# Attention of all 49 tiles in a loop of its own in the first ten steps, its result and the input kept in place of the tile's transposed input

## The reference

```
Wh  = xn @ W + b;  gnn[d] = mean of Wh[src] over the 100000 edges with that dst       (graph part)
q,k = elu(xn @ wq + bq) + 1, elu(xn @ wk + bk) + 1;  v = xn @ wv + bv                 (8 heads of 32)
mix = (q @ (k^T v)) / (q . sum(k) + 1e-6) @ wo + bo                                   (linear attention)
x1  = x + gnn + mix
out = x1 + expert MLP of layernorm(x1)     (top 1 of 8 experts, 256 -> 1024 -> 256, capacity 977, softmax weight)
```

## Time and profile before

| | |
|---|---|
| median of 3 runs | 1505.08 us |
| the profiled execution | 1504.29 us |
| its span | 1502.5 us |
| mean granted TensorE clock | 0.875 |
| TensorE matmuls busy | 1147.8 us (76%) |
| GpSimd busy | 961.9 us (64%) |
| VectorE busy | 833.8 us (55%) |
| ScalarE busy | 558.1 us (37%) |

### The profile page before, as it was taken

One profiled execution on the slowest core, in us unless ns is written; L12 is line 12 of the kernel. 1 busy time (PEld: TensorE's weight loads), 2 busy tenths in 40 slices (PEclk: granted clock), 3 DMA queues, 4 the chain that ended last, 5 costly groups with the idle time before them and its releaser, 6 DMA issues.

```text
span 1502.5 us, 33191 instructions
## 1 busy us (share of the span) xinstructions
PE 1147.8 (76%) x5962; PEld 790.6 (53%) x5963; DVE 833.8 (55%) x3074; ACT 558.1 (37%) x1460; POOL 961.9 (64%) x969
## 2 busy tenths in 40 slices
PE   3779876456565556588888888988899999988796
PEld 2557543122222223365656656666666767767685
DVE  6755333033233235356566766777777777776454
ACT  4832211011111113243434544555444545554342
POOL 5447777777777767777776776767767767611111
PEclk9589997566677668899999999999999999999898
DMA  7583334344344443545455554555555545534452
GB/s 238 190 263 99 104 101 134 102 131 133 103 148 143 135 123 114 166 142 168 143 174 174 178 171 138 176 169 168 183 181 182 188 156 177 164 101 132 136 182 84
DMA packets 141735, 228.94 MB, mean 152 GB/s; under 512 B 29856, under 2 KB 86723, under 8 KB 141618
## 3 DMA queue, kind: packets, MB, share of 16 engines
q0 software_dynamic: 42800, 115.65, 25.2%
q1 hardware_dynamic: 97454, 111.65, 23.5%
q10 hardware_dynamic: 1364, 0.54, 0.2%
HBM read 194.65 MB, written 34.81 MB: 153 GB/s over the span
## 4 chain that ended last, share of the span: by engine, by line
PE 29%; POOL 27%; issue 27%; DMA 6%; POOLq 4%; DVE 3%; ACT 2%; SPq 1%; ACTq 0%; DVEq 0%; PEldq 0%
POOL shared L594 26%; PE pY L1055 7%; PE pH L1064 7%; PE pA L935 5%; DMA shared<-table,idx 4%; PE pQ L1001 1%; PE pX L1032 1%; PE pX L1028 1%; DMA shared<-in_L_ffn_b_dram 1%; PE pX L1030 1%; PE pD L938 1%; PE pH L912 1%; DMA shared<-in_x_dram 1%; POOLq L554 1%; POOLq L562 1%
## 5 line engine op out<-in xcount | busy, mean ns | idle before, releaser
L594 POOL DMA_INDIRECT shared<-table,idx x784 | 811.3, 1035 | 299.4 <-issue 255.2
L935 PE MATMUL pA<-shared,onehot 128*128 x976 | 304.1, 442 | 238.4 <-POOLq L571 173.3
L935 PEld LDWEIGHTS pA<-shared,onehot 128*128 x976 | 102.5, 105 | 429.4 <-issue 381.4
L1055 PE MATMUL pY<-w2s,shared 128*128 x832 | 196.6, 390 | 11.9 <-issue 9.0
L1064 PEld LDWEIGHTS pH<-shared 128*128 128x128 f32 x1664 | 193.9, 192 | 2.6
L1064 PE MATMUL pH<-shared 128*128 128x128 f32 x1664 | 194.3, 275 | 0.0
L707 ACT ACTIVATE shared<-pA,rdeg 128x256 f32<-128x256 f32 x49 | 23.2, 473 | 437.0 <-DVE rdeg L1493 433.1
L1055 PEld LDWEIGHTS pY<-w2s,shared 128*128 128x128 f32 x832 | 157.0, 194 | 33.9 <-issue 13.7
L1481 DVE CUSTOM_DVE_ANT_1 pD<-pD,ident 128x512 f32<-128x512 f32 x49 | 34.3, 700 | 210.9 <-PE pD L941 198.7
L772 ACT ACTIVATE shared<-pH,b1s 128x128 f32<-128x128 f32 x416 | 116.2, 371 | 49.6 <-PE pH L1064 47.0
L531 POOL DMA_INDIRECT out_dram<-shared,jtok x52 | 55.7, 1072 | 114.0 <-issue 114.0
(11 more groups left out here) (275 smaller groups left out, 1744.0 us busy)
## 6 DMA issues: line engine op xcount, KB each, us to landing
shared<-in_L_ffn_w_dram SPq DMA_DIRECT2D x104, 512.0 KB
shared<-table,idx POOLq DMA_INDIRECT x784
w2s<-in_L_ffn_w_dram SPq DMA_DIRECT2D x8, 1024.0 KB, 6.5
rows<-rows_sb SPq DMA_DIRECT2D x7, 1040.0 KB, 14.9
shared<-rows SPq DMA_DIRECT2D x52, 130.0 KB
shared<-in_L_ffn_b_dram SPq DMA_DIRECT2D x52, 128.0 KB
shared<-in_x_dram SPq DMA_DIRECT2D x12, 512.0 KB, 8.7
table<-w2s SPq DMA_DIRECT2D x12, 512.0 KB, 3.5
```

What stands on the lines that cost most here:

```text
L594: g.indirect_dma_start(gathered[:, s * G + j, :], None, table[:, :], bass.IndirectOffsetOnAxis(ap=idx[:, q * G + j:q * G + j + 1], axis=0) ...
L935: m = pe.matmul(pA[:, :], onehot[:, n % OQ, j, :], groups[:, f % RQ, j, :], start=False, stop=stop)
L1055: ins = pe.matmul(pY[:, 0:D], hs[:, c, :], w2s[:, bass.ds(e * FC * D + c * D, D)], start=(c == 0), stop=(c == FC - 1))
```

## The change

The attention leaves the steps of its tiles. It runs in a loop of its own, `attend`, six tiles in each of the steps 0 to 4, four in each of 5 to 8, and the last three in step 9. TensorE does query(b+1), divisor(b), the projection of tile b-1 (`mixed`, which takes the bias and the `ms` matmuls out of `project_sum`), and spread(b). ScalarE does the Relu of b+1, the divisors' copy of b behind the projection of b-1, and the Exp of b+1. VectorE adds the projection to the input tile and keeps it in the tile's place in `xts` (`attended`), which isn't needed any more, adds the 8 gate columns to `xgs`, and does qn and qf. The banks change: divisors to pH0, spread to pH1, projection to pY, which no job uses yet. Input tiles come in pairs into a part of `hs`, which jobs use from step 10 on, and `xres` is gone. In a step with attention, VectorE's `place` and `combine` stand ahead of it and the next tile's one-hots behind it; TensorE's attention stands between `count` and `turn_sums`. The core of the diff:

```diff
+SIX = 5
...
+        xpair = hs[:, 0:2 * DK, :].rearrange("p (a c) n -> p a (c n)", a=2)
...
-        xres = part_of(D)
...
+        def attended(t):
+
+            return xts[:, bass.ds(t, 1), :, :].rearrange("p t k n -> p (t k n)")
...
+            def load_res(a, par, first=False):
+
+                if not first:
+                    sp.wait_ge(S["at_ok"], a)
...
+            with sp.Fori(1, SIX) as t:
+                load_pairs(3 * t, 3 * t + 3)
                 step(t, False, False, False)
                 load_out_weights(t)
+            with sp.Fori(SIX, T0 - 2) as t:
+                load_pairs(2 * t + SIX, 2 * t + (SIX + 2))
+                step(t, False, False, False)
+                load_out_weights(t)
...
+            def attend(b):
+
+                more = not isinstance(b, int) or b + 1 < NT
+                if more:
+                    a.wait_ge(S["qf_ok"], b + 1)
                     a.sem_inc(S["act_hold"], 1)
+                    a.wait_ge(S["q_ps"], b + 2)
+                    query_part(qr, ACT.Relu)
+                a.wait_ge(S["rd_ok"], b + 1)
                 a.sem_inc(S["act_hold"], 1)
+                if not isinstance(b, int) or b >= 1:
+                    a.wait_ge(S["at_ps"], b)
+                    a.sem_inc(S["act_hold"], 1)
                 each = rden[:, :].rearrange("p (h a) -> p h a", a=1).broadcast_to([P, HEADS, HD])
                 a.activation(qn.rearrange("p (h d) -> p h d", h=HEADS), each, ACT.Copy).then_inc(S["dn_ok"], 1)
+                if more:
+                    query_part(qe, ACT.Exp).then_inc(S["qe_ok"], 1)
...
+                def mixed(t):
+
+                    pe.wait_ge(S["qn_ok"], t + 1)
+                    pe.sem_inc(S["pe_hold"], 1)
+                    pe.wait_ge(S["at_ok"], t + 1)
+                    pe.sem_inc(S["pe_hold"], 1)
+                    pe.matmul(pY[:, 0:GW], qn[:, 0:P], ms[:, 0, :], start=True, stop=False)
+                    pe.matmul(pY[:, 0:D], two16[:, :], bo16[:, :], start=False, stop=False)
+                    pe.matmul(pY[:, 0:GW], qn[:, P:D], ms[:, 1, :], start=False, stop=True).then_inc(S["at_ps"], 1)
+
+                def attend(b):
+
+                    inner = not isinstance(b, int)
+                    if inner or b + 1 < NT:
+                        pe.wait_ge(S["qe_ok"], b + 1)
+                        pe.sem_inc(S["pe_hold"], 1)
+                        query(b + 1).then_inc(S["q_ps"], 1)
+                    divisor(b)
+                    if inner or b >= 1:
+                        mixed(b - 1)
+                    spread(b)
...
-                    pe.matmul(pX[:, 0:GW], st[:, 0:P], wgs[:, 0, :], start=True, stop=False)
-                    pe.matmul(pX[:, 0:D], two16[:, :], bo16[:, :], start=False, stop=False)
-                    pe.matmul(pX[:, 0:GW], st[:, P:D], wgs[:, 1, :], start=False, stop=False)
                     for m in range(DK):
-                        ins = pe.matmul(pX[:, 0:GW], qn[:, m * P:(m + 1) * P], ms[:, m, :], start=False, stop=(m == DK - 1))
+                        ins = pe.matmul(pX[:, 0:GW], st[:, m * P:(m + 1) * P], wgs[:, m, :], start=(m == 0), stop=(m == DK - 1))
...
+                def keep(t, landed_at, par):
+
+                    v.wait_ge(S["at_ps"], t + 1)
+                    hold(v, "dve_hold")
+                    v.wait_ge(S["xo_in" if par else "xe_in"], landed_at)
+                    hold(v, "dve_hold")
+                    v.tensor_tensor(attended(t), pY[:, 0:D], xpair[:, par, :], ALU.add)
+                    at = xgs[:, bass.ds(t, 1), :].rearrange("p t n -> p (t n)")
+                    v.tensor_tensor(at, pY[:, D:GW], at, ALU.add).then_inc(S["at_ok"], 1)
+
+                def attend(i, par):
+
+                    t = 2 * i + par
+                    inner = not isinstance(t, int)
                     k = part("share_c", t)
+                    v.wait_ge(S["den_ps"], t + 1)
+                    hold(v, "dve_hold")
+                    k(v.tensor_scalar(rden[:, :], pH0[:, 0:HEADS], 1e-6, None, ALU.add))
                     assert k.n == K["share_c"]
                     v.reciprocal(rden[:, :], rden[:, :]).then_inc(S["rd_ok"], 1)
+                    if inner or t >= 1:
+                        keep(t - 1, i * 16 + 16 if par else i * 16, 1 - par)
                     v.wait_ge(S["qf_ok"], t + 1)
                     hold(v, "dve_hold")
                     v.wait_ge(S["rx_ps"], t + 1)
                     hold(v, "dve_hold")
+                    v.tensor_tensor(qn, qf, pH1[:, 0:D], ALU.mult).then_inc(S["qn_ok"], 1)
+                    if inner or t + 1 < NT:
+                        queries(t + 1)
...
+                    if pairs:
+                        if inner or t >= 2:
+                            place(t - 2)
+                        combine(t)
...
+                            attend_pairs(*pairs)
...
                     if inner or t + 1 < NT:
                         next_tile(t)
```

More of the change, by code:

```diff
@@ L363, in _, with load_pairs @@
             sp.dma_start(bgb, gnn_b.partition_broadcast(P)).then_inc(S["bg_in"], 16)
[L364 to L371, removed]
-                else:
-                    sp.dma_start(xres, x_t[bass.ds(t, 1), :, :].rearrange("t p d -> p (t d)")).then_inc(S["xr_in"], 16)
+            def load_res(a, par, first=False):
+                if not first:
+                    sp.wait_ge(S["at_ok"], a)
+                    hold(sp, "sp_hold")
+                name = "xo_in" if par else "xe_in"
+                if isinstance(a, int) and a == NT - 1:
+                    sp.dma_start(xpair[0:LAST, par, :], x[(NT - 1) * P:N, :]).then_inc(S[name], 16)
+                else:
+                    sp.dma_start(xpair[:, par, :], x_t[bass.ds(a, 1), :, :].rearrange("t p d -> p (t d)")).then_inc(S[name], 16)
+            def load_pairs(lo, hi):
+                with sp.Fori(lo + 1, hi + 1) as i:
+                    load_res(2 * i, 0)
+                    load_res(2 * i + 1, 1)
             def store_x1(t, last=False):
@@ L774, in hidden, with step @@
                     ins.then_inc(S["h_sb"], 1)
-            def step(t, turn=True, work=True, out_=True):
+            def step(t, turn=True, work=True, out_=True, pairs=None):
                 inner = not isinstance(t, int)
@@ L782, in step @@
                     count_on(t)
[L783 to L786, removed]
+                if pairs:
+                    if isinstance(t, int) and t == 0:
+                        attend(0)
+                        attend(1)
+                        attend_pairs(1, pairs[1])
+                    else:
+                        attend_pairs(*pairs)
+                    if isinstance(t, int) and t == T0 - 1:
+                        attend(NT - 1)
                 if turn:
@@ L797, in step @@
                     softmax(t - 1)
[L799 to L803, removed]
+            a.wait_ge(S["q_ps"], 1)
+            query_part(qr, ACT.Relu)
+            query_part(qe, ACT.Exp).then_inc(S["qe_ok"], 1)
+            step(0, False, False, False, (0, 3))
+            with a.Fori(1, SIX) as t:
+                step(t, False, False, False, (3 * t, 3 * t + 3))
+            with a.Fori(SIX, T0 - 1) as t:
+                step(t, False, False, False, (2 * t + SIX, 2 * t + (SIX + 2)))
+            step(T0 - 1, True, False, False, (2 * (T0 - 1) + SIX, (NT - 1) // 2))
             step(T0, True, True, False)
@@ L1094, in step @@
                         ins.then_inc(S["px_ps"], 1)
-                    if inner or t < NT:
-                        pe.wait_ge(S["qf_ok"], t + 1)
-                        pe.sem_inc(S["pe_hold"], 1)
-                        if inner or t + 1 < NT:
-                            query(t + 1)
-                        divisor(t).then_inc(S["qd_ps"], 1)
+                    if pairs:
+                        if isinstance(t, int) and t == 0:
+                            attend(0)
+                            attend(1)
+                            attend_pairs(1, pairs[1])
+                        else:
+                            attend_pairs(*pairs)
+                        if isinstance(t, int) and t == T0 - 1:
+                            attend(NT - 1)
+                            mixed(NT - 1)
+                            pe.wait_ge(S["at_ok"], NT + 1)
                     if out_:
@@ L1620, in step @@
                         node_out(t - 1)
-                    if inner or t < NT:
-                        divisors(t)
-                    if inner or t >= 2:
+                    if not pairs:
                         place(t - 2)
```

116 lines of the change are left out of this document (62 added, 54 removed).

## The result

The changed kernel takes **1582.2 us** (median of 4 runs, 1575.7 to 1589.8) against 1506.5 before: ratio 1.049, 95% interval 1.046 to 1.052. It is slower where 1483 us was forecast, outside the range, and of the other sign.

The account below looks back on a forecast made before the run. GpSimd's issue of gathers was taken to bound the first ten steps and nearly the next 14 tiles, TensorE the last 24. Early +44, middle -15, late -48, tail -2 gave -21 us from 1504.3: 1483 us, range 1454 to 1522.

Parts of the forecast that it names:

- So I take 2.4 GHz: Early attention loop: TensorE at work 2.9 of 4.4 us, a larger share than in an earlier stretch, so full clock.
- rival (b): Early attention loop: TensorE falls to 1.2 GHz, trips of 5.9 us, +69 us, 1552 us in all; chance 0.05.
- The round trip, 4.4 us: Early steps: each further attention costs one pass round three engines, 4.4 us, ends 4.1 and 5.0.
- (a): Early attention loop: dearer handovers, trips of 5.3 us, early stage 41 us more, 1524 us in all; chance 0.21.
- The end of a loop: Early steps: VectorE's last two products, leaving the loop and the next tile's one-hots keep TensorE waiting 3.8 us.
- Late steps: Last 24 tiles: TensorE loses 2.7 us a step, to 14.8 or 16.4; VectorE bounds three-group steps at 15.8.
- The term of -48: Last 24 tiles: 383 us in place of 431, 48 us less.
- GpSimd's 362 us stay below: Last 24 tiles: GpSimd needs 272 x 1.33 = 362 us, less than the 383 us forecast for the stage.
- The -15 of the middle stage: Tiles 10 to 24: GpSimd sets the pace at 291 of 306 us, so only its 15 us can go.
- The tail: Behind the last node sum, mostly expert jobs: 147.2 us becomes 145, a change of -2 us.
- (d): Late steps hardly shrink since VectorE keeps 17 us: 12 us saved in place of 48, 1519 us; chance 0.04.
- (c): Early attention hides better behind GpSimd, 4.0 us each: early stage costs 20 in place of 44, 1459 us; chance 0.13.

Follow-up runs that it names:

- e1: Changed kernel with two matmuls on zeros per attention, filling TensorE's wait for ScalarE: 1544.2 us, ratio 1.026.
- e2: Changed kernel with a job's weights loaded ahead of the next job's rows in SP's queue: 1586.4 us, ratio 1.052.
- e17: Changed kernel in which GpSimd sends out no finished job inside the steps, 39 instructions less: 1573.7 us, ratio 1.045.
- e4: Changed kernel with the divisors' copy in its own buffer and VectorE's addition to the input behind the next query: 1518.7 us, ratio 1.009.
- e18: Changed kernel with the whole attention left out, VectorE only copying the input tiles: 1477.2 us, ratio 0.981.
- e5: Changed kernel with each group's rows scattered three groups behind its gathers instead of five: 1613.9 us, ratio 1.069.

## Why the prediction was wrong

**"So I take 2.4 GHz"** failed first. The forecast argued from one stretch of the earlier trace rows, where TensorE was at work for 3.06 of 6.8 us at 2.4 GHz, that a larger share of work would hold that clock. The stretches above show that share says little: at 1.2 GHz TensorE was at work for 29.4 of 33.0 us, at 2.4 GHz for 17.6 of 22.8. Of 39 trips between two spreads of one loop 19 took over 6 us. That is 19 x 2.1 = 40 us, and e1 gave back 38. e2 and e17 have 20 and 19 such trips, but partly in other steps: which loops fall to 1.2 GHz isn't fixed by the step. It is rival (b), given 0.05, in half of the trips. (b) was sized as +69 for all steps with trips of 5.9 us; they took 6.7. The Trainium skill (TensorE: Matmul & The Clock Gate, section "A second HAM failure mode: psum-queue depth-cycling") had warned of short idles between groups of matmuls. The loops at 1.2 GHz bear out its warning, but not its picture of a clock that swings between the levels as the idles recur: here it kept one level for five trips on end in steps 0, 3 and 4, and changed within a loop in steps 1, 2 and 9.

**The round trip, 4.4 us**, was well built. Measured 4.56: divisors 0.44 for 0.37, the projection to ScalarE's start 1.68 for 1.54, then to the spread 0.56 (0.56), to L1550 0.55 (0.54), from there to L1522 0.75 for 0.56, to the next divisors 0.57 (0.54); the 0.3 for handovers is in these. The query's 1.22 for 0.97 lies beside it. The forecast counts a trip 46 times, but its own steps hold 39 behind the first attention of each, so in the ends of its range and in the sizes of (a) and (b) the trips weigh a sixth too much; 0.16 x 39 = 6 us were missed here. **The end of a loop**, 3.8 us from the first of VectorE's two last products to the first group, was 4.8 (L1550 at 474.19, L972 at 479.02): 10 us in ten steps. Part of both came back in the groups behind, 12.2 us for 13.1 in step 3. The four steps at 2.4 GHz throughout (3, 4, 6, 8) took 158.7 us where the forecast has 154.6, and with the filler all ten took 437.3 for 423. So 38 of the 52 us at tile 10 are the clock, and 14 are what is left with the clock held: trips and ends above their price.

**"Late steps"**: the 2.7 us of TensorE were right (14.90 measured for 14.8; 16.7 to 17.3 for 16.4). VectorE's 15.8 us as the next bound was wrong: it kept up with 14.9. The term of -48 failed by another step: **"GpSimd's 362 us stay below"**. In the last stage GpSimd is busy for 299.8 us, and 0.30 us stand between two of its 274 instructions: 382 us in which it waits for nobody, 10 more than the 372 of TensorE. It isn't below; it is the slower of the two. Its instructions are dearer here (1.09 us busy) than in the early stretch from which 1.33 us each was taken (211.04 / 210, 1.00 us). The difference sits in 23 of its 267 indirect transfers: they took 1.87 to 3.13 us, each of them beside one of VectorE's 24 one-hots (L1489, 2.29 us), and the other 244 took 0.98. That is 36 us; in the last stage of the kernel before it is 18 transfers and 22 us. Two engines near one pace, a few groups of ring between them, and a scatter that one of them issues between gathers: waits stay, and 382 became 415. How these 33 us of waits arise is argued from the chain above, and no run takes them away: in e1, e4 and e18 GpSimd's sum is 375 to 378 us and the stage 410 to 413. The forecast named TensorE waiting for rows or expert weights behind GpSimd's scatters as a thing that would be wrong, but priced it at nothing. In e17, with GpSimd at 259.2 + 248 x 0.30 = 334 us, 19 us came back; in e5, with the scatter moved, the wait moved too.

**The -15 of the middle stage** became -8, and this though TensorE came into it with a full ring, which is worth 12 us (310.4 in e18, 298.3 after) and with which the forecast had 282. The step that failed is "only its 15 us can go": by GpSimd's own pace nothing went. It needs 222.45 + 213 x 0.30 = 286 us there without a wait, so its 291 were about right; but it waits for another 12 us, in e18 for 20, before for 17. The rows name no releaser for most of it, and ten instructions fewer changed nothing (step 14 of e17), so why it stays is open.

**The tail** was right: 144.4 for 145.

Rival (a) had the place right and not the reason: the 39 trips took 5.6 us on average, above its 5.3, but by the clock, and at 2.4 GHz handovers left them at 4.56, below its 4.9. (d) had the size of the late stage nearly right (12 where 16 came) by a mechanism that isn't there, and (c) did not come. No version here beats the kernel before: the best, e4, is 0.9% slower, and the ceiling with no attention at all is 1.9% below it, 6 us under the forecast. A forecast that sits at the ceiling of its own idea should have been a warning.

## What to carry to other kernels

Price a stage by every engine's need in that stage, from rows of the same stage, not from another, and look which of its instructions run beside an instruction of another engine that makes them longer. Where the relieved engine comes down to the pace of a second one, the waits between them take what is left of the gain. A chain that goes round three engines costs a handover on each leg, and its matmuls may run at half the clock although TensorE is busy for 9 parts in 10. Filling its gaps gave 38 us (e1); shortening it gave the same and 24 us more (e4). Before moving work, ask what the kernel would take if that work cost nothing.

## What the runs showed of the hardware

- TensorE kept 1.2 GHz through loops in which it was busy 89% of the time (29.37 of 33.00 us), and 2.4 GHz through loops of the same instructions at 77%. Two matmuls on zeros a trip took every trip but the first to 2.4 GHz.
- The same program took 1506 to 1509 us on four groups of runs and 1758 to 1770 us on two, each on another chip. On the slow ones TensorE and VectorE stood by issue for up to 25 us in the early steps; why, no run shows. Without results sent the changed kernel was 8.5 and 9.0% above the kernel before there, and 4.5% on the other chip.
- In the last 24 steps 244 of GpSimd's 267 indirect transfers took 0.98 us on average and the other 23 took 1.87 to 3.13, all of these beside VectorE's one-hots. VectorE's timeline beside the scatter of 3.13 us in step 28:

```profile
1089.15 2.29 DVE L1489 TENSOR_TENSOR onehot<-node_ids,dst_t 128x2048 f16 x1 [0.17 <-issue]
```

  The Trainium skill (SBUF — State Buffer, section "SBUF: two separate sides") speaks of a port that VectorE and GpSimd share and that one of them holds alone for a whole instruction. The rows agree: the scatter starts with the one-hots and ends 0.9 us behind them. No run here takes the one-hots away.
